# A reordered step in the last stage: z, y, d, covariance on TensorE, and h's low half ahead of g on VectorE

## The reference

```python
# layer 0: p = clip(u.T @ (relu(x) - mean)), quantised to 256 levels by the channel's range
p = jnp.matmul(u.T, im - mn);  p = jnp.clip(p, -cv, cv)
q = round((p - dmin) * scale) / scale + dmin
x = jnp.matmul(u, q) - mean + mn
# layer 1, for each sample
out = relu(bn(einsum('oc,bchw->bohw', w_conv1, x)))       # 256 -> 256
d   = relu(bn(einsum('oc,bchw->bohw', w_dr, out) + b_dr)) # 256 -> 128
cov = einsum('bim,bjm->bij', xc, xc) / M                  # xc: d less its mean over positions
r   = einsum('cjh,bch->bcj', w_row, bn(cov)) + b_row
att = sigmoid(einsum('oc,bc->bo', w_fc, r) + b_fc)
return x * att                                            # x is layer 0's output
```

## Time and profile before

| | |
|---|---|
| median of three runs | 2001.55 us |
| the profiled execution | 2002.28 us, span 2000.3 us |
| last stage | from about 869 us to the end |
| TensorE busy (pipelined matmuls) | 1683.9 us of the span |
| VectorE, ScalarE busy | 1471.1 us, 1425.2 us |
| GpSimd | works in the first stage only |
| DMA in the span | 438.6 MB, 219 GB/s |
| matmuls of the last stage in the whole: z, y | 1792 each |
| matmuls of d | 4800 |

### The profile page before, as it was taken

How to read it: one execution, slowest core, us unless ns; L and a number is a source line. 1 busy time by engine, 2 the same in 40 slices (tenths; PEclk the granted TensorE clock), 3 DMA queues, 4 the chain that set the end, 5 groups by cost and what they waited for, 6 DMA issues and landing times.

```text
span 2000.3 us, 39033 instructions
## 1 busy us (share of the span) xinstructions
PE 1683.9 (84%) x13394; PEld 1317.5 (66%) x13394; DVE 1471.1 (74%) x2633; ACT 1425.2 (71%) x2046; POOL 460.3 (23%) x135
## 2 busy tenths in 40 slices
PE   8999999999942000059999999999999999999998
PEld 8999999999931000036666666666666666666664
DVE  6888888888865443358878787777778787777774
ACT  6777777777755775646777777777777777777776
POOL 7888888888810000000000000000000000000000
PEclk9999999999965555579999999999999999999999
DMA  9999989989968999920423223242423223242414
GB/s 333 374 350 336 372 313 371 369 313 377 371 280 339 391 424 424 423 84 17 161 81 140 100 108 132 80 161 80 161 80 142 99 111 130 80 161 80 161 66 194
DMA packets 95806, 438.60 MB, mean 219 GB/s; under 512 B 8480, under 2 KB 9632, under 8 KB 80672
## 3 DMA queue, kind: packets, MB, share of 16 engines
q1 hardware_dynamic: 95776, 438.21, 57.1%
HBM read 219.82 MB, written 218.37 MB: 219 GB/s over the span
## 4 chain that ended last, share of the span: by engine, by line
PE 50%; DVE 5%; issue 1%; ACT 0%; DMA 0%; DVEq 0%
PE y_ps L836 15%; PE z_ps L786 14%; PE d_ps L816 14%; PE cov_ps L800 4%; DVE hl L961 2%; DVE g L947 1%; DVE gg L953 1%; PE ch_ps L844 1%; PE ch_ps L826 0%; DVE gg L955 0%; PE ch_ps L827 0%; DMA q<-q_scratch 0%; PE cov_ps L803 0%; ACT yo L895 0%; DVEq L989 0%
## 5 line engine op out<-in xcount | busy, mean ns | idle before, releaser
L268 POOL TENSOR_TENSOR xl<-xs,xh 128x1568 fp32r<-128x1568 f32 x128 | 459.4, 3590 | 97.2 <-ACT xh L228 97.2
L895 ACT ACTIVATE yo<-y_ps,att_cy 128x512 f32<-128x512 f32 (+2 forms) x448 | 313.9, 723 | 138.8 <-PE y_ps L836 128.0
L867 ACT ACTIVATE h<-z_ps,sb_h 128x512 f32<-128x512 f32 (+2 forms) x448 | 277.1, 634 | 73.5 <-PE z_ps L786 63.6
L786 PE MATMUL z_ps<-qr,wh 128*128 128x512 f16 (+2 forms) x896 | 314.4, 354 | 1.4 <-DVE qr L913 1.4
L836 PE MATMUL y_ps<-qr,udh 128*128 128x512 f16 (+2 forms) x896 | 313.5, 353 | 2.3 <-ACT yo L895 1.8
L786 PE MATMUL z_ps<-qr,wl 128*128 128x512 f16 (+2 forms) x896 | 314.2, 354 | 0.0
L836 PE MATMUL y_ps<-qr,udl 128*128 128x512 f16 (+2 forms) x896 | 313.0, 352 | 0.0
L228 ACT ACTIVATE xh<-xs 128x1568 fp32r<-128x1568 f32 x128 | 194.2, 1517 | 140.1 <-PE pp L285 140.0
L816 PE MATMUL d_ps<-vh,hh 128*128 128x128 f16 (+1 forms) x1600 | 282.3, 220 | 10.4 <-DVE hl L961 10.4
L947 DVE SCALAR_TENSOR_TENSOR g<-d_ps,late 128x512 f32<-128x512 f32 (+1 forms) x224 | 141.9, 634 | 198.6 <-PE d_ps L816 194.8
L816 PE MATMUL d_ps<-vh,hl 128*128 128x128 f16 (+1 forms) x1600 | 281.0, 219 | 0.0
(11 more groups left out here) (158 smaller groups left out, 2716.1 us busy)
## 6 DMA issues: line engine op xcount, KB each, us to landing
xs<-in_x_dram SPq DMA_DIRECT2D x128, 784.0 KB, 6.8
out_dram<-yo SPq DMA_DIRECT2D x31, 3136.0 KB, 9.2
pt<-p_scratch SPq DMA_DIRECT2D x56, 1568.0 KB, 11.0
p_scratch<-po_low SPq DMA_DIRECT2D x56, 784.0 KB, 7.8
p_scratch<-late SPq DMA_DIRECT2D x56, 784.0 KB, 7.8
q<-q_scratch SPq DMA_DIRECT2D x32, 784.0 KB, 5.0
q_scratch<-qt SPq DMA_DIRECT2D x28, 784.0 KB, 11.4
q_scratch<-q_res SPq DMA_DIRECT2D x8, 392.0 KB, 11.9
```

Of the source, the lines that this page charges most:

```text
L268: nc.gpsimd.tensor_tensor(xl[:, k % 2], xs[:, k], xh[:, k % 2].bitcast(F32), ALU.subtract).then_inc(split_done, 1)
L786: last = nc.tensor.matmul(z_ps[:, m, 0:w], part[:, k, m * P:(m + 1) * P], qr[:, a, k, columns(s)], start=k == 0 and part is wh, stop=k == ...
L867: nc.scalar.activation(h32[:, par, m, 0:w], z_ps[:, m, 0:w], ACT.Relu, bias=sb_h[:, m:m + 1]).then_inc(z_read, 1)
L895: nc.scalar.activation(yo[:, slot, m, columns(c)], y_ps[:, m, 0:widths[c]], ACT.Identity, scale=att_cy[:, m, 0:1], bias=att_cy[:, m, 1:2]) ...
```

## The change

TensorE's blocks of a step become local functions and their order becomes z, spread, y, logits, d, covariance. In step 1 covariance keeps its place behind z, since it is the last chunk of the sample before, and VectorE's reading of the covariance waits for it. VectorE's order becomes: reading the covariance, centring, weighting, conversion, hl, g. The first operation of g now also waits for the g before it to be split, since g32 has one buffer.

```diff
@@ TensorE
-                        if has(r2, a, s, 2):
-                            ... (covariance, in place)
-                        if has(r2, a, s, 1):
-                            ... (d, in place)
-                        ... (spread, y, logits, in place)
+                        if s == 1:
+                            covariance(r2, a, s)
+                        spread(r2, a, s)
+                        outputs(r2, a, s)
+                        logits(r2, a, s)
+                        reduced(r2, a, s)
+                        if s != 1:
+                            covariance(r2, a, s)
@@ VectorE: g and hl move from ahead of the centring to behind the conversion, hl first
                             convert(a if s + LEAD < CH else 1 - a, c)
+                        if exists(r2, a):
+                            w = widths[s]
+                            dve.wait_ge(hh_done, g + 1)
+                            nc.vector.tensor_tensor(hl[:, par, :, 0:w], h32[:, par, :, 0:w], hh[:, par, :, 0:w],
+                                                    ALU.subtract).then_inc(h_split, 1)
+                        if has(r2, a, s, 1):
+                            dw = widths[(s - 1) % CH]
+                            dt, dq = -(-dw // P), min(P, dw)
+                            dve.wait_ge(d_done, g)
+                            wait_from(dve, g_split, g - 1)
+                            nc.vector.scalar_tensor_tensor(out=g32[0:dq, 0:dt], in0=d_ps[0:dq, 1 - par, 0:dt],
+                                                           scalar=1.0 / LIFT, in1=nb[0:dq, 0:dt], op0=ALU.mult,
+                                                           op1=ALU.max).then_inc(d_read, 1)
+                            ... (the split of g as before)
```

More of the change, by code:

```diff
@@ L773, in _, with covariance @@
                 pe.wait_ge(weights_done, 1)
+                def covariance(r2, a, s):
+                    g = first_chunk(r2, a) + s
+                    if has(r2, a, s, 2):
+                        c, par = (s - 2) % CH, (CH * a + s) % 2
+                        pe.wait_ge(g_split, g - 1)
+                        if c == 0:
+                            wait_from(pe, cov_read, 2 * r2 + a)
+                        for t in range(tiles[c]):
+                            q = min(P, widths[c] - t * P)
+                            end = c == CH - 1 and t == tiles[c] - 1
+                            nc.tensor.matmul(cov_ps[:, 0:2 * P + 1], gg[0:q, par, t, 0:P],
+                                             gg[0:q, par, t, 0:2 * P + 1], start=c == 0 and t == 0,
+                                             stop=False)
+                            last = nc.tensor.matmul(cov_ps[:, 2 * P:2 * P + 1], gg[0:q, par, t, P:2 * P],
+                                                    gg[0:q, par, t, 2 * P:2 * P + 1], start=False, stop=end)
+                        last.then_inc(cov_done, 1)
@@ new lines, in reduced @@
+                def reduced(r2, a, s):
+                    g = first_chunk(r2, a) + s
+                    if has(r2, a, s, 1):
+                        c, par = (s - 1) % CH, (CH * a + s - 1) % 2
+                        pe.wait_ge(h_split, g)
+                        wait_from(pe, d_read, g - 2)
+                        for t in range(tiles[c]):
+                            q = min(P, widths[c] - t * P)
+                            parts = [(hx[:, par, k, t * P:t * P + q], vx[:, k])
+                                     for k in range(K) for hx, vx in ((hh, vh), (hh, vl), (hl, vh))]
+                            for n, (lhs, rhs) in enumerate(parts):
+                                last = nc.tensor.matmul(d_ps[0:q, par, t], lhs, rhs, start=n == 0,
+                                                        stop=n == len(parts) - 1)
+                        last.then_inc(d_done, 1)
@@ new lines, in spread @@
+                def spread(r2, a, s):
+                    n = 2 * r2 + a
+                    if s == 2 and exists(r2, a, back=1):
+                        pe.wait_ge(diag_done, n)
+                        pe.wait_ge(hl_copied, n)
+                        wait_from(pe, att_done, n - 1)
+                        nc.tensor.matmul(ch_ps[:, 0:P], hl_sb[:], ident[:], start=True, stop=True)
+                        nc.tensor.matmul(ch_ps[:, P:2 * P], ones[:], dg[:], start=True,
+                                         stop=True).then_inc(spread_done, 1)
@@ new lines, in outputs @@
+                def outputs(r2, a, s):
+                    if has(r2, a, s, CH + Y_LAG):
+                        o, slot, c = output_chunk(r2, a, s)
+                        for m in range(K):
+                            pe.wait_ge(y_free, K * o + m + 1)
+                            for k in range(K):
+                                for part in (udh, udl):
+                                    last = nc.tensor.matmul(
+                                        y_ps[:, m, 0:widths[c]], part[:, k, m * P:(m + 1) * P],
+                                        qr[:, slot, k, columns(c)],
+                                        start=k == 0 and part is udh, stop=k == K - 1 and part is udl)
+                            last.then_inc(y_done, 1)
@@ L775, in phase, with logits @@
+                def logits(r2, a, s):
+                    n = 2 * r2 + a
+                    if s == Y_LAG and exists(r2, a, back=1):
+                        pe.wait_ge(weighted_done, J * n)
+                        for m in range(K):
+                            last = nc.tensor.matmul(ch_ps[:, 2 * P + m:2 * P + m + 1], weighted[:, m],
+                                                    ones[:, 0:1], start=True, stop=True)
+                        last.then_inc(logits_done, 1)
                 def phase(r2, a):
@@ L941, in phase @@
                             nc.vector.tensor_tensor(a_sb[:], cov_ps[:, 0:P], hl_sb[:], ALU.add).then_inc(cov_read, 1)
[L942 to L962, removed]
                         if s == 2 and exists(r2, a, back=1):
```

7 lines of the change are left out of this document (added).

## The result

The changed kernel takes 1989.03 us, the median of six runs (1985.05 to 1993.33), against 2002.20 us for the kernel before in six runs on the same chip. The ratio estimated from these executions is 0.9927, with a 95% interval from 0.9914 to 0.9941 (the two medians alone give 0.9934), so it is faster by 0.7%. The forecast was 1985.6 us, with 1981.5 to 1994.0 as its range. The profiled execution took 1993.33 us, its span 1991.4.

A forecast was written before the change was run, and what follows sets the result against it. TensorE's own work bounds the steady part, apart from one wait; a circle of d, g and hl bounds the first samples. Terms -9.9 - 6.7 + 0.7 = -15.9 us took the profiled 2002.28 to a median of 1985.6; range 1981.5 to 1994.

The forecast's parts named there:

- What bounds it: Last stage: steady part bound by TensorE's own work plus one 0.33 us wait a sample; first samples by a circle.
- (1): Steady part, step 3 of a sample: d's 0.33 us wait for hl goes, 9.9 us over 30 samples.
- (3): TensorE's transitions between blocks: spread's first load may hide better, 0 to 0.1 us a sample, taken as 0.
- (2): Covariance in step 1: g ready after 6.69 us, TensorE there at 6.82, lead 0.13, so no wait; range 0 to 0.33.
- The estimate of 2 us: Covariance in step 1: cost in all if the skill's load time and full drain held; weighed, not adopted.
- (4): First two samples of the last stage: the circle through g and hl opens, 39.9 us for 46.6, 6.7 saved.
- (5): After the last z: covariance waits 1.5 us for g, blocks take 8.6 us for 7.86, 0.7 us lost.
- A: Rival, step 1: the wait moves to covariance, 0.2 to 0.33 us a sample, 9.9 given back, 1995.5 us; 8%.
- B: Rival, first samples: another circle is found and the start gives nothing, 1992.3 us; 5%.
- C: Rival, step 1: ScalarE reaches h(0) late, hl(0) holds VectorE, g 1.5 us late a sample, 2031 us; 4%.
- 0.2% (4 us): Whole kernel: about what a measurement can tell from no change; faster by more than this was given 0.93.

The follow-up runs named there:

- full_d: Changed kernel with d of a sample's last tile made on all 128 positions in place of 64: 1982.00 us, ratio 0.9879 to the kernel before.
- after_pair: The changed kernel again, no edit, six executions beside the last experiments: median 1986.57 us, ratio 0.9905 to the kernel before; profiled execution 1986.38 us.
- before_a: The kernel before again, no edit, one profiled execution: 2010.57 us, with the slow second stage (312.8 us) and a clock fall in the end.
- after: The changed kernel's first profiled execution, no further edit: 1993.33 us, with a clock fall in the end.
- after_again: The changed kernel again, no edit, five executions: median 1986.19 us, ratio 0.9900 to the kernel before; profiled execution 1991.75 us, no clock fall in the end.
- pe_only: TensorE's new order alone, VectorE's order as in the kernel before: 2069.51 us, ratio 1.0303 to the kernel before.
- dve_only: VectorE's new order alone, TensorE's order as in the kernel before: 2167.32 us, ratio 1.0803 to the kernel before.

## Why the prediction was right, step by step

**What bounds it.** Right. The steady part was TensorE's own blocks plus one wait, and blocks read from start to start kept their length in the new order (z 1.72, d 1.34, covariance 0.55).

**(1) and (3), the steady part.** The mechanism held, and the wait went. The size was short by a fifth: 0.40 us a sample, 12.1 for 30, where 0.33 and 9.9 stood. From z to z only two steps changed (means of 24 samples): TensorE's step 4, where d of chunk 3 waited, from 5.63 to 5.28, and step 2, with the spread, from 5.42 to 5.36. The term that was mis-sized is the spread's in step (3), which I took as 0 and bounded by 0.1: its fp32 matmuls take 0.44 behind z (1219.04 to 1219.48) and took 0.50 behind the 128-column d. The last 0.01 is in step 4 as well: d took 1.35 behind the load that had waited, and takes 1.34 now. The rows of the spread and of y behind it in the changed kernel:

```profile
1219.04 0.38 PE L817 MATMUL ch_ps<-ident,hl_sb 128*128 128x128 f32 x2
1219.48 0.33 PE L829 MATMUL y_ps<-qr,udh 128*128 128x384 f16 x1
```

**(2) What is late next.** Right: no wait. On the mean the split ends at 6.65 us and a load that waits for it starts 0.05 later (as in `full_d`), together 6.70 for 6.69 in the sum; TensorE is there at 6.82, so the lead is 0.12 for 0.13. By sample it lies between 0.07 and 0.17, because g of three tiles takes 1.73 to 1.82 us where the sum had 1.74; that the thinnest still holds was not worked out. `full_d` then had TensorE there 0.21 earlier and got a wait of 0.11 on the mean. What was weighed there is now tested on a covariance. The Trainium skill's "TensorE: Matmul & The Clock Gate", section LDWEIGHTS (loading the stationary operand), gives 107 ns for a load of 128 columns. The load's own row agrees (0.10 at 1483.81 in `full_d`), but it isn't paid: load and matmul both start at 1483.81, 0.05 after g was split (1483.20 + 0.56), and the block of covariance takes 0.58 behind it for 0.57 in the changed kernel. The Trainium skill's "VectorE: DVE Perf Modes", section The DRAIN you can't avoid, has the next operation wait until the pipeline is empty; the same section of the Trainium skill adds that one that isn't held back starts earlier. g starts at 1212.15, 0.09 before hl's 1211.01 + 1.23, so the trace agrees with the addition. The estimate of 2 us, which took a bare load and the full drain, didn't come.

**(4) The start.** Right: -6.8 for -6.7, and no single step is off by more than 0.07. In `after_pair` the first step is 3.80 for 3.6 and the whole start 39.91, so the steps repeat less well than their sum. Walking two in-order queues from durations of rows was enough.

**(5) The end.** The blocks are right, +0.7. What wasn't foreseen is the clock. After waits of 1.34 and 1.83 us TensorE ran at 1.2 GHz for 3.4 us, which cost 1.6. The kernel before has the 1.83 us wait in its end in all three profiles and the fall in one (`before_a`); the changed kernel has both waits in all three and the fall in two. So the waits don't settle it alone. Of all thirteen profiles, seven have both waits in their end, and five of them the fall; of the six without covariance's wait three have it. Whether the change makes the fall more likely these few profiles can't say.

**The rivals.** A is refuted by the missing row and by 34.197 in every profile; but by only 0.12 us, as `full_d` shows. B is refuted by the start. C is refuted by the same rows as A: hl(0) started 1.55 us after VectorE's last work, released by hh, and ScalarE wasn't late. Its kind of mistake, one queue holding up the other, is what the two half changes have.

**The total.** 1989.03 is 3.4 above the forecast. By parts, in the profiled run: -0.7 from the last stage, +6.9 from the second, +0.8 from the first. The error lies in a stage that the change doesn't touch, and which I took as fixed from a single profile. That the median of six came as near as 3.4 is in part luck: it depends on how many of the six had the quick pace. The statement that 0.2% (4 us) can be told from no change is true only between executions of one pace of the second stage, or over many executions; one execution is off by 6.9 us by that alone. In the changed kernel's later runs the medians were 1986.19 and 1986.57, near the forecast; more executions at the quick pace would explain that, but only one of each had a profile.

## What to carry to other kernels

Read a change's gain between marks inside its own stage, start to start, and not from the total: here the last stage repeats to a hundredth of a us a sample, while a stage that isn't touched moves the total by 7. When two in-order queues feed each other, move the consumer and the producer together and walk both queues on from rows; half a reorder gave 3% and 8% of loss where the whole gave 0.7 to 1% of gain. And when a wait is removed, work out how far the next one lies, since a later saving ahead of it (0.21 here) is only partly paid (0.10) until that one is moved as well.

## What the runs showed of the hardware

- The same DMA-bound stage took 305.2 to 307.5 us in nine profiles and 311.3 to 313.3 in four, at 420 to 425 or 393 to 400 GB/s in the window from 790 to 830 us, whatever the kernel.
- TensorE's granted clock fell from 2.4 to 1.2 GHz for about 3.4 us in the end, while it still had work, in eight of the thirteen profiles, behind a wait of 1.83 us, for some 1.5 us of time (36.01 us from the last z to the end in `after`, 34.52 in `after_again`); in the other five it did not, with the same wait in each. With about 1.7 us of waits in each sample of 37 us (`pe_only`) it fell again about every 146.8 us, and with about 4 us of waits a sample (`dve_only`) 19 times before the last z. In the eleven other profiles, with 0.35 us a sample or less, it stayed at 2.4 GHz from 883 us to the last z.
- A 64-position tile behind full ones cost d 0.21 us more than if the tile were full (1.22 against 1.01), most of it in two pauses of 0.15 us where the shape changes.
- The fp32 spread is 0.06 us shorter behind a z of 512 columns than behind d of 128.
- A weight load that had to wait for its operand started together with its first matmul (1483.81) and cost 0.01 us: d took 1.35 behind it for 1.34, covariance 0.58 for 0.57.
